# A message stage over 128 pairs of 512 edges under one mask, in place of 232 pairs of 256 edges under four

## The chip, the cores and the metric

The kernel runs on one core of a Trainium2 chip. The metric is the device time of one execution in microseconds (us). TensorE is called PE, VectorE DVE, ScalarE ACT, GpSimd POOL and SyncE SP in the profile.

## What is computed

The whole program is a graph layer, a mixture-of-experts layer, a second graph layer and a second expert layer over 3125 nodes of 256 features, with 53125 edges sorted by their destination. The change concerns the second graph layer's messages:

```
xg0 = y0[edge_src]                       # 64 scalars of the source node
xg1 = y1[edge_src]                       # 64 vectors of 3 components
ea0 = edge_attr[:, :1]
ea1 = edge_attr[:, 1:4]
mid0 = w_a * xg0 * ea0
mid1 = w_b * einsum("euc,ec->eu", xg1, ea1) * INV_SQRT3
mid2 = (w_c * xg0)[:, :, None] * ea1[:, None, :]
mid3 = (w_d * ea0)[:, :, None] * xg1
agg  = segment_sum(concatenate([mid0, mid1, mid2, mid3]), edge_dst)
```

w_a to w_d are 64 weights each per edge, made from edge scalars. Per edge the message has 8 x 64 = 512 values, and they are summed per destination node.

## The kernel before

The stages run one after the other with a barrier between them (times from the profiled span): `sum_neighbours` (0 to 543 us; the first graph layer's sum over neighbours, and the edge weights w with the attributes behind them, 260 columns per edge, written to memory as `edge_w`), the first layer's matmuls and experts (to 1069), `sum_messages` (to 1631), and the update with the second experts (to the end). Nodes lie in 25 tiles of P = 125; the sum over a tile's edges is a matmul on PE whose stationary operand is a mask (edge on the partition, node of the tile in the column).

`sum_messages`. Edges are taken in blocks of SB = 256 (KC = 2 chunks of 128 on the partitions), NB = 208 blocks. A block can touch two tiles, so the work is a list of NPAIR = 208 + 24 = 232 (block, tile) pairs; the tables `pair_need` (the block), `pair_tile` and `pair_dst` (per edge the node's place in the tile) are worked out on the chip at the start of `sum_neighbours`. Two pairs (four chunks) make a step, NST = 116 steps. All operands are float32, and the trace shows every float32 matmul as two instructions. In a step:
- SP loads two blocks of weights `msg_w` (L1939), into RS = 4 buffers.
- POOL fetches the source nodes' 256 values with one indirect DMA per chunk, `msg_got` (L1963): 416 of them, one after the other, into a ring of 32 blocks, at most 7 blocks ahead of the pairs whose products are made (semaphore `made`).
- DVE makes the mask of the next step (`msg_plain`, L2016, 4 x 125 columns, comparing a row of node numbers in PSUM with `pair_dst`), then per pair three products into `msg_prod`: 256 columns (L2033: first and last weight group times the scalars) and twice 384 (L2035: the two middle groups times the vectors). Three steps behind it adds the two sums from PSUM into `agg` (L2045, 512 columns each, second behind first by the semaphore `added`).
- ACT multiplies the mask of each chunk by each of three attributes: 12 masks `msg_scaled` of 125 columns (L1984).
- PE multiplies plain mask by 256 columns of products (L2001) and the three scaled masks by 128 columns each (L2005), per chunk.

In the buffers of `msg_w`, `msg_plain`, `msg_scaled` and `msg_prod` one is borrowed from `x_sb`, so the trace also has the name `x_sb` in their place.

The tables. After the sorted edges' counts are known, DVE builds the pair tables with three trips to PE (L504 to L517 on PE, L833 to L858 on DVE). Then come the row statistics of the nodes (L814, L817 and L821, "gathered statistics"), of which the one-hot masks and the edge work of that stage follow. In that stage POOL's gathers (L441) of block b >= 32 wait for PE's sum of an earlier pair (L556).

## Time and profile before

| what | us |
|---|---|
| median of 3 runs | 1990.52 |
| lowest, highest run | 1987.57, 1991.15 |
| the profiled execution | 1992.24 |
| its span in the trace | 1990.5 |
| first stage, message stage in the span | 0 to 543, 1069 to 1631 |
| PE, DVE, ACT, POOL busy over the span | 1761.1, 1125.7, 1021.4, 1109.6 |
| mean granted TensorE clock | 0.938 |

The trace is of one execution; it takes 1.7 us more than the median of the runs and 1.7 more than its own span. In the rows below an operation's duration runs from its start to the end of its write, and the next of the same engine can begin before that; the difference of two starts is what an operation takes of the engine.

### The profile page before, as it was taken

To read this page: it belongs to the slowest core of one execution; us is meant where nothing else is said; L and a number is where in the kernel's file an instruction comes from. 1 tells how busy PE (TensorE), PEld (TensorE's weight loads), DVE (VectorE), ACT (ScalarE), POOL (GpSimd) and SP (SyncE) were. 2 spreads that over 40 slices of the span, in tenths; PEclk is the share of its full clock that TensorE was granted. 3 is DMA by queue.
4 is the path that set the end of the run, shared out by engine and by line. 5 is a ranking of instruction groups with operands and counts; after the bars stand their busy time and mean duration, and the time that the engine had idled before them with its cause. 6 is when DMAs were issued, how large, how long until landed. Compare 5 with 4: busy or idle time off the path is not lost. (4 is left out here: it accounts for less than half of the span.)

```text
span 1990.5 us, 38467 instructions
## 1 busy us (share of the span) xinstructions
PE 1761.1 (88%) x9911; PEld 1434.7 (72%) x9911; DVE 1125.7 (57%) x2792; ACT 1021.4 (51%) x3052; POOL 1109.6 (56%) x1499
## 2 busy tenths in 40 slices
PE   2799999999899839999755999999999999995999
PEld 1466666666566729999634899888999887774887
DVE  6644333333411665544494999999999973233122
ACT  5455545555443612322246777777777745552221
POOL 6788888888600014555347888888888830000343
PEclk7899999999999559999977999999999999996999
DMA  8767777778640246667456777777777761564553
GB/s 235 221 214 248 246 238 242 242 238 266 210 153 0 65 103 213 208 212 217 148 126 204 210 218 215 215 214 218 216 213 218 209 172 52 172 188 116 177 176 120
DMA packets 229316, 376.43 MB, mean 189 GB/s; under 512 B 66200, under 2 KB 114427, under 8 KB 229117
## 3 DMA queue, kind: packets, MB, share of 16 engines
q1 hardware_dynamic: 174908, 222.13, 36.8%
q0 software_dynamic: 52224, 150.15, 25.2%
q10 hardware_dynamic: 1984, 1.79, 0.3%
q8 instruction: 89, 1.46, 0.3%
q14 instruction: 111, 0.90, 0.1%
HBM read 275.38 MB, written 99.57 MB: 188 GB/s over the span
## 5 line engine op out<-in xcount | busy, mean ns | idle before, releaser
L1963 POOL DMA_INDIRECT msg_got<-y_dram,block_src x416 | 417.9, 1004 | 101.7 <-issue 93.2
L441 POOL DMA_INDIRECT ffn_w<-xn_dram,block_src x384 | 364.4, 949 | 96.0 <-issue 87.5
L1984 ACT ACTIVATE msg_scaled<-msg_plain,msg_w 128x125 f32<-128x125 f32 x1044 | 312.0, 386 | 95.2 <-DVE msg_plain L2016 95.2
L556 PEld LDWEIGHTS sum_ps_bank<-ffn_w,sum_onehot 128*125 128x125 f32 x928 | 171.6, 193 | 191.1 <-issue 175.4
L556 PE MATMUL sum_ps_bank<-ffn_w,sum_onehot 128*125 x928 | 254.3, 399 | 50.0 <-DVE sum_onehot L898 26.1
L886 DVE TENSOR_TENSOR agg<-sum_ps_bank,agg 125x256 f32 x232 | 98.6, 425 | 282.9 <-PE sum_ps_bank L556 278.4
L655 ACT ACTIVATE sum_space<-sum_ps_bank,sum_rec 128x128 f32<-128x128 f32 x416 | 130.1, 364 | 202.1 <-PE sum_ps_bank L543 200.4
L543 PE MATMUL sum_ps_bank<-sum_fc,sum_space 128*128 128x512 f32 x416 | 211.5, 593 | 1.3 <-ACT sum_space L644 1.3
L2005 PEld LDWEIGHTS msg_ps_z<-msg_prod,msg_scaled 128*125 128x125 f32 x1416 | 174.5, 189 | 6.8
L2005 PE MATMUL msg_ps_z<-msg_prod,msg_scaled 128*125 128x128 f32 x1416 | 175.2, 274 | 0.0
L2045 DVE TENSOR_TENSOR agg<-msg_ps_z,agg 125x512 f32 x232 | 159.8, 689 | 22.0 <-DVE agg L2045 1.8
L1538 ACT ACTIVATE ffn_run_hid<-ffn_run_ps_h,cols 128x128 f32<-128x128 f32 x256 | 73.0, 368 | 179.2 <-PE ffn_run_ps_h L1495 179.2
L2462 POOL DMA_INDIRECT last_rows<-ffn_rows,ffn_token x32 | 30.8, 962 | 231.8 <-SPq L78 222.4
L2001 PE MATMUL msg_ps_z<-msg_prod,msg_plain 128*125 128x256 f32 x472 | 126.9, 392 | 20.2 <-ACT msg_scaled L1984 10.8
L1495 PEld LDWEIGHTS ffn_run_ps_h<-ffn_run_rows_t,ffn_run_w 128*128 128x128 f32 x1024 | 125.9, 194 | 5.0 <-DVE ffn_run_rows_t L1580 1.8
L1495 PE MATMUL ffn_run_ps_h<-ffn_run_rows_t,ffn_run_w 128*128 128x128 f32 x1024 | 126.6, 278 | 1.0 <-DVE ffn_run_rows_t L1580 1.0
L1600 POOL DMA_INDIRECT ffn_results<-ffn_run_res,ffn_place x64 | 66.5, 1038 | 102.0 <-DVE ffn_run_res L1559 102.0
L1509 PE MATMUL ffn_run_ps_r<-ffn_w,ffn_run_hid 128*128 x512 | 121.0, 380 | 0.0
L1984 ACT ACTIVATE x_sb<-x_sb 128x125 f32<-128x125 f32 x348 | 104.0, 386 | 33.1 <-DVE x_sb L2016 33.1
L2035 DVE TENSOR_TENSOR msg_prod<-msg_w,msg_got 128x384 f32<-128x384 f32 x236 | 120.4, 551 | 0.1
L2423 PE MATMUL last_ps_r<-wd,last_hid_t 128*128 x512 | 117.7, 384 | 0.0
L2001 PEld LDWEIGHTS msg_ps_z<-msg_prod,msg_plain 128*125 128x125 f32 x472 | 80.2, 190 | 36.1 <-issue 15.3
(346 smaller groups left out, 3252.5 us busy)
## 6 DMA issues: line engine op xcount, KB each, us to landing
edge_w<-sum_space SPq DMA_DIRECT2D x52, 1040.0 KB, 5.2
msg_w<-edge_w SPq DMA_DIRECT2D x174, 260.0 KB
ffn_run_w<-in_L_ffn_w SPq DMA_DIRECT2D x64, 512.0 KB
x_sb<-edge_w SPq DMA_DIRECT2D x58, 260.0 KB
ffn_rows<-agg SPq DMA_DIRECT2D x25, 448.0 KB
ffn_w<-in_L_ffn_w SPq DMA_DIRECT2D x16, 512.0 KB, 8.7
wd<-in_L_ffn_Wd SPq DMA_DIRECT2D x8, 1024.0 KB, 8.9
msg_got<-y_dram,block_src POOLq DMA_INDIRECT x416, 3.7
```

The lines of the kernel that those rows point to most:

```text
L441: pool.indirect_dma_start(got[:, (b + 1) % RING, u, :], None, k.x if b < RAW else k.xn_dram, bass.IndirectOffsetOnAxis(ap=k.block_src[:, b ...
L543: pe.matmul(ps_w[q % WB][:, :, :].rearrange("p u d -> p (u d)"), hid[g % 2][:, b, :], fc2[:, :, :, :].rearrange("p u k v -> p (u k v)"), s ...
L556: last = pe.matmul(ps_sum[n % ZB][0:P, :], onehot[n % OB][:, u, :], got[:, ds(need % RING, 1), u, :].rearrange("p o d -> p (o d)"), start= ...
L655: act.activation(to[:, b, u, 0:128], ps_w[q % WB][:, u, 0:128], ACT.Copy, scale=r[:, b, u, 8:9])
L1495: last = pe.matmul(ps_h[b][c // 4][:, c % 4, :], w1[s][:, q, c * 128:(c + 1) * 128], rows_t[b][:, q, :], start=(q == 0), stop=(q == 1))
L1509: last = pe.matmul(ps_r[b][:, :], hid[b][:, c, :], m.w2[:, ds(e, 1), c, :].rearrange("p o d -> p (o d)"), start=(c == 0), stop=(c == HC - 1))
L1963: pool.indirect_dma_start(got[:, (b + 1) % RING, u, :, :].rearrange("p k v -> p (k v)"), None, k.y_dram, bass.IndirectOffsetOnAxis(ap=k.bl ...
L1984: last = act.activation(scaled[s % MB][:, x, c, :], plain[s % MB][:, c, :], ACT.Copy, scale=w[s % RS][:, c, D + x:D + x + 1])
L2001: pe.matmul(z[0:P, 0:4, :], mask[:, c, :], p[:, c, 0:4, :], start=(u == 0), stop=False, skip_group_check=True)
L2005: last = pe.matmul(z[0:P, 4:6 + x:1 + x, :], by[:, x, c, :], p[:, c, 4 + x:8:3 - x, :], start=False, stop=(x == 2 and u == KC - 1), skip_g ...
L2035: last = dve.tensor_tensor(p[:, at, 3 * q - 2:3 * q + 1, :], v[:, at, q:q + 1, :].to_broadcast([128, KC, 3, MUL]), y[:, :, 1:4, :], ALU.mult)
L2045: dve.tensor_tensor(row(k.agg, tile), ps_z[n % ZB][0:P, :, :].rearrange("p k v -> p (k v)"), row(k.agg, tile), ALU.add)\
```

## The change

Blocks of the message stage are now 512 edges (four chunks): NB4 = 104 blocks, NP4 = 104 + 24 = 128 pairs, and each pair is one unit of work. There is one mask per chunk, the plain one that DVE makes, and PE multiplies it by all 512 columns of products in one matmul of one bank (L2079 in the changed file). What the scaled masks did is done on the products:
- For the three column groups of mid2, ACT copies the product w_c times scalars (64 columns per chunk) three times with an attribute as scale: 12 copies of 64 columns (`split`), in place of 12 masks of 125.
- For mid1, DVE multiplies vectors by attributes in one operation of 768 columns into a new buffer `msg_along` (L2106), adds the three components (two adds of 256 columns, L2113 and L2116), and multiplies by w_b (256 columns, L2120). These wait for one another with the semaphore `along_made`.
- For mid3, one product of 768 columns (L2114); mid0 and the input of the split, one of 512 (L2104).

The add into `agg` is one of 512 columns per unit (L2127), three units behind. POOL's gathers are the same 416, into a ring of 16 four-chunk blocks; it waits only every 8 blocks, for the unit `block4_done` says. SP has one DMA per unit. The memset of agg's first half is moved ahead of the wait for the row of node numbers. The tables for 104 blocks and 128 pairs are made from the old ones' counts in `sum_neighbours`, before the first gathered statistics; PE's edge work and ACT's copies of edge attributes now wait for them (`tables_made` 4). The old tables live on as buffers of that stage only.

```diff
--- before.py
+++ after.py
+NB4 = NB // 2
+NP4 = NB4 + T - 1
+CH = 2 * KC
+RING4, HOLD4 = 16, 8
...
+            pe.wait_ge(four_ready, 5)
+            for h in range(2):
+                pe.matmul(ps_four[:, h:h + 1], ranks.rearrange("p k j -> p (k j)"), minus[:, h:h + 1], start=True, stop=(h == 0))
+            pe.matmul(ps_four[:, 1:2], k.ones[:, :], minus[:, 0:1], start=False, stop=True)
...
+            pe.wait_ge(shifted, 4)
+            pe.wait_ge(chosen_made, 6)
+            for c in range(CH):
+                for h, (at, n) in enumerate(HALVES):
+                    last = pe.matmul(ps_field4[:, c, :], dst_fb[h][0:n, :, c % KC], chosen_half[c // KC][0:n, h, :],
+                                     start=(h == 0), stop=(h == 1))
+            last.then_inc(field_ready, 1)
...
+                        pe.wait_ge(tables_made, 4)
...
+            chain(dve.tensor_tensor(tile4_row[0:1, :], ps_rows4[0:1, 128:128 + NP4], k.iota[0:1, 0:NP4], ALU.add))
+            dve.tensor_scalar(k.pair4_need[0:1, :], ps_rows4[0:1, 0:NP4], float(NB4 - 1), 1.0, ALU.min, ALU.add).then_inc(step, 1)
+            dve.tensor_scalar(k.pair4_tile[0:1, :], tile4_row[0:1, :], float(T - 1), None, ALU.min).then_inc(tables_made, 1)
+            done[0] += 1
+            dve.tensor_copy(k.block4_done[0:1, :], ps_rows4[0:1, 256:256 + NB:2]).then_inc(tables_made, 1)
+            dve.wait_ge(field_ready, 2)
+            dve.scalar_tensor_tensor(k.pair4_dst[:, :, :].rearrange("p n c -> p c n"),
+                                     k.iota[:, 0:NP4].unsqueeze(1).to_broadcast([128, CH, NP4]), float(-P),
+                                     ps_field4[:, :, :], ALU.mult, ALU.add).then_inc(tables_made, 1)
+            dve.wait_ge(tables_made, 4)
...
-            for s in range(NST):
-                if s >= RS:
-                    sp.wait_ge(made, s - RS + 1)
-                    sp.wait_ge(scaled_made, s - RS + 1)
-                if s == 1:
+            for n in range(NP4):
+                if n >= RS:
+                    sp.wait_ge(made, n - RS + 1)
+                    sp.wait_ge(split_made, n - RS + 1)
+                if n == 1:
                     sp.wait_ge(k.x_put, 32 * (NG - 1))
-                for h in range(2):
-                    n = 2 * s + h
-                    need = sp.value_load(k.pair_need[0:1, n:n + 1], min_val=1, max_val=NB)
-                    sp.dma_start(w[s % RS][:, KC * h:KC * h + KC, :].rearrange("p u w -> p (u w)"),
-                                 k.edge_w[ds((need - 1) * SB, SB), :].rearrange("(p u) w -> p (u w)", u=KC)).then_inc(w_in[s % RS], 16)
+                need = sp.value_load(k.pair4_need[0:1, n:n + 1], min_val=1, max_val=NB4)
+                sp.dma_start(w[n % RS][:, :, :].rearrange("p (h u) w -> p h (u w)", h=2),
+                             k.edge_w[ds((need - 1) * (2 * SB), 2 * SB), :].rearrange("(h p u) w -> p h (u w)", h=2, u=KC))\
+                  .then_inc(w_in[n % RS], 16)
...
-                if b > AHEAD:
-                    pool.wait_ge(made, (b - AHEAD + 1) // 2)
+                if b >= 2 * RING4 and b % (2 * HOLD4) == 0:
+                    last = b // 2 - HOLD4 - 1
+                    done = pool.value_load(k.block4_done[0:1, last:last + 1], min_val=1, max_val=NP4)
+                    pool.wait_ge(made, done)
+                    pass_on(pool, freed)
                 for u in range(KC):
                     pool.indirect_dma_start(
-                        got[:, (b + 1) % RING, u, :, :].rearrange("p k v -> p (k v)"), None, k.y_dram,
-                        bass.IndirectOffsetOnAxis(ap=k.block_src[:, b, u:u + 1].bitcast(U32), axis=0)).then_inc(got_in[b % RING], 16)
+                        got[:, (b // 2 + 1) % RING4, b % 2 * KC + u, :, :].rearrange("p k v -> p (k v)"), None, k.y_dram,
...
-            for s in range(NST):
-                act.wait_ge(masked, s + 1)
-                act.wait_ge(w_in[s % RS], 32 * (s // RS + 1))
-                if s >= MB:
-                    act.wait_ge(summed, s - MB + 1)
+
+            def split(n):
+                act.wait_ge(w_in[n % RS], 16 * (n // RS + 1))
+                act.wait_ge(opened, n + 1)
+                p = prod[n % XB]
                 for c in range(CH):
                     for x in range(3):
-                        last = act.activation(scaled[s % MB][:, x, c, :], plain[s % MB][:, c, :], ACT.Copy,
-                                              scale=w[s % RS][:, c, D + x:D + x + 1])
-                last.then_inc(scaled_made, 1)
+                        last = act.activation(p[:, c, 5 + x, :], p[:, c, 8, :], ACT.Copy, scale=w[n % RS][:, c, D + x:D + x + 1])
+                last.then_inc(split_made, 1)
+
+            for n in range(NP4):
+                split(n)
 
         @block.tensor
         def _(pe):
             pe.matmul(ps_lanes[:, :], k.onesf[0:1, :], k.iota[0:1, 0:P], start=True, stop=True).then_inc(lanes_made, 1)
-            for s in range(NST):
-                pe.wait_ge(scaled_made, s + 1)
-                pe.wait_ge(made, s + 1)
-                if s >= ZB // 2:
-                    pe.wait_ge(added, 1 + 2 * (s - ZB // 2 + 1))
-                mask, by, p = plain[s % MB], scaled[s % MB], prod[s % XB]
-                for h in range(2):
-                    z = ps_z[(2 * s + h) % ZB]
-                    for u in range(KC):
-                        c = KC * h + u
-                        pe.matmul(z[0:P, 0:4, :], mask[:, c, :], p[:, c, 0:4, :], start=(u == 0), stop=False, skip_group_check=True)
-                    for x in range(3):
-                        for u in range(KC):
-                            c = KC * h + u
-                            last = pe.matmul(z[0:P, 4:6 + x:1 + x, :], by[:, x, c, :], p[:, c, 4 + x:8:3 - x, :],
-                                             start=False, stop=(x == 2 and u == KC - 1), skip_group_check=True)
+            for n in range(NP4):
+                pe.wait_ge(masked, n + 1)
+                pe.wait_ge(made, n + 1)
+                pe.wait_ge(split_made, n + 1)
+                if n >= ZB:
+                    pe.wait_ge(added, 1 + n - ZB + 1)
+                for c in range(CH):
+                    last = pe.matmul(ps_z[n % ZB][0:P, :, :], plain[n % MB][:, c, :], prod[n % XB][:, c, 0:8, :],
+                                     start=(c == 0), stop=(c == CH - 1))
                 last.then_inc(summed, 1)
 
         @block.vector
         def _(dve):
-            def mask(s):
-                if s == 1:
+            def place(n):
+                return dve.value_load(k.pair4_need[0:1, n:n + 1], min_val=1, max_val=NB4)
+
+            def mask(n):
+                if n == 1:
                     dve.wait_ge(k.x_put, 32 * (NG - 1))
-                if s >= MB:
-                    dve.wait_ge(summed, s - MB + 1)
-                dve.tensor_tensor(plain[s % MB][:, :, :], ps_lanes[:, :].unsqueeze(1).to_broadcast([128, CH, P]),
-                                  k.pair_dst[:, 2 * s:2 * s + 2, :].rearrange("p n u -> p (n u)").unsqueeze(2)
-                                  .to_broadcast([128, CH, P]), ALU.is_equal).then_inc(masked, 1)
-
-            def place(n):
-                return dve.value_load(k.pair_need[0:1, n:n + 1], min_val=1, max_val=NB)
-
-            def products(s, need):
-                p = prod[s % XB]
-                v = w[s % RS][:, :, 0:D].rearrange("p c (k v) -> p c k v", v=MUL)
-                dve.wait_ge(w_in[s % RS], 32 * (s // RS + 1))
-                dve.wait_ge(blocks_in, need[1])
-                if s >= XB:
-                    dve.wait_ge(summed, s - XB + 1)
-                for h in range(2):
-                    y = got[:, ds(need[h] % RING, 1), :, :, :].rearrange("p o u k v -> p (o u) k v")
-                    at = slice(KC * h, KC * h + KC)
-                    dve.tensor_tensor(p[:, at, 0:8:7, :], v[:, at, 0:4:3, :], y[:, :, 0:1, :].to_broadcast([128, KC, 2, MUL]), ALU.mult)
-                    for q in (1, 2):
-                        last = dve.tensor_tensor(p[:, at, 3 * q - 2:3 * q + 1, :], v[:, at, q:q + 1, :].to_broadcast([128, KC, 3, MUL]),
-                                                 y[:, :, 1:4, :], ALU.mult)
-                last.then_inc(made, 1)
+                if n >= MB:
+                    dve.wait_ge(summed, n - MB + 1)
+                dve.tensor_tensor(plain[n % MB][:, :, :], ps_lanes[:, :].unsqueeze(1).to_broadcast([128, CH, P]),
+                                  k.pair4_dst[:, n, :].unsqueeze(2).to_broadcast([128, CH, P]), ALU.is_equal).then_inc(masked, 1)
+
+            def open_products(n, need):
+                p, t = prod[n % XB], along[n % TB]
+                v = w[n % RS][:, :, 0:D].rearrange("p c (k v) -> p c k v", v=MUL)
+                y = got[:, ds(need % RING4, 1), :, :, :].rearrange("p o c k v -> p (o c) k v")
+                dve.wait_ge(w_in[n % RS], 16 * (n // RS + 1))
+                dve.wait_ge(blocks_in, need)
+                if n >= XB:
+                    dve.wait_ge(summed, n - XB + 1)
+                dve.tensor_tensor(p[:, :, 0:9:8, :], v[:, :, 0:4:3, :], y[:, :, 0:1, :].to_broadcast([128, CH, 2, MUL]), ALU.mult)\
+                   .then_inc(opened, 1)
+                dve.tensor_tensor(t[:, :, :, :], y[:, :, 1:4, :],
+                                  w[n % RS][:, :, D:D + 3].unsqueeze(3).to_broadcast([128, CH, 3, MUL]), ALU.mult).then_inc(along_made, 1)
+                return v, y
+
+            def close_products(n, v, y):
+                p, t = prod[n % XB], along[n % TB]
+                dve.wait_ge(along_made, 3 * n + 1)
+                dve.tensor_tensor(t[:, :, 0, :], t[:, :, 0, :], t[:, :, 1, :], ALU.add).then_inc(along_made, 1)
+                dve.tensor_tensor(p[:, :, 1:4, :], v[:, :, 1:2, :].to_broadcast([128, CH, 3, MUL]), y[:, :, 1:4, :], ALU.mult)
+                dve.wait_ge(along_made, 3 * n + 2)
+                dve.tensor_tensor(t[:, :, 0, :], t[:, :, 0, :], t[:, :, 2, :], ALU.add).then_inc(along_made, 1)
+                if n + 1 < NP4:
+                    mask(n + 1)
+                dve.wait_ge(along_made, 3 * n + 3)
+                dve.tensor_tensor(p[:, :, 4, :], v[:, :, 2, :], t[:, :, 0, :], ALU.mult).then_inc(made, 1)
```

DVE in the message stage of the kernel before, one step from its mask to the next: L2060 and L2021 (L2139 and L2086 in the changed file) are loads of table entries into registers, ISA rows are register instructions; rows that repeat are left out.

```order
L2016 TENSOR_TENSOR msg_plain<-msg_ps_lanes,pair_dst 128x500
L2033 TENSOR_TENSOR msg_prod<-msg_w,msg_got 128x2x2x64
L2035 ISA
L2035 TENSOR_TENSOR msg_prod<-msg_w,msg_got 128x2x192 x2
L2060 TENSOR_LOAD pair_tile
L2021 TENSOR_LOAD pair_need
L2021 ISA x2
L2045 ISA
L2045 TENSOR_TENSOR agg<-msg_ps_z,agg 125x512
```

(The second and third row stand there twice, once per pair, and the last row too.) The same engine in the changed kernel, one unit from its first product:

```order
L2104 TENSOR_TENSOR msg_prod<-msg_w,msg_got 128x4x2x64
L2106 ISA
L2106 TENSOR_TENSOR msg_along<-msg_got,msg_w 128x768
L2086 TENSOR_LOAD pair_need
L2086 ISA x2
L2127 ISA
L2127 TENSOR_TENSOR agg<-msg_ps_z,agg 125x512
L2113 TENSOR_TENSOR msg_along<-msg_along 128x4x64
L2114 TENSOR_TENSOR msg_prod<-msg_w,msg_got 128x4x192
L2116 TENSOR_TENSOR msg_along<-msg_along 128x4x64
L2093 TENSOR_TENSOR msg_plain<-msg_ps_lanes,pair_dst 128x500
L2120 TENSOR_TENSOR msg_prod<-msg_w,msg_along 128x4x64
```

Six products of 256 and 384 columns, two adds and a mask for two pairs have become eight operations for one unit, with the add now in the middle of it and the next mask ahead of the last product.

DVE in the first stage of the kernel before, where the tables end and the gathered statistics begin:

```order
L870 CAST iota_h<-sum_space 128x256
L814 BN_STATS ffn_w<-ffn_w 128x6 x4
L817 BN_AGGR ffn_w<-ffn_w 128x2 x4
L814 BN_STATS ffn_w<-ffn_w 128x6 x4
L817 BN_AGGR ffn_w<-ffn_w 128x2 x4
L821 RECIPROCAL ffn_w<-ffn_w 128x4
```

The same place in the changed kernel, its last part; between the cast of iota_h and these rows stand 14 others with two of the three trips to PE:

```order
L935 SCALAR_TENSOR_TENSOR sum_space<-iota,sum_space 128x128 x2
L937 TENSOR_SCALAR sum_space<-sum_space 128x2
L939 TENSOR_SCALAR sum_space<-sum_space 128x256
L939 TENSOR_SCALAR sum_space<-sum_space 80x256
L941 TENSOR_SCALAR sum_space<-sum_space 128x256
L943 TENSOR_TENSOR sum_space<-sum_space 128x256
L945 TENSOR_TENSOR sum_space<-sum_ps_bank,iota 1x128
L946 TENSOR_SCALAR pair_need<-sum_ps_bank 1x128
L947 TENSOR_SCALAR pair_tile<-sum_space 1x128
L949 CAST block_done<-sum_ps_bank 1x104
L951 SCALAR_TENSOR_TENSOR pair_dst<-iota,sum_ps_bank 128x4x128
L855 BN_STATS ffn_w<-ffn_w 128x6 x4
```

The statistics of L814 (now L855) have moved behind all of them.

## Rows read from the trace of the kernel before

**Rows 1.** Windows: stretch; length, busy us (count) per engine; PEclk, DMA share, GB/s
```profile
core 0: us, PE busy (x) PEld busy (x) DVE busy (x) ACT busy (x) POOL busy (x), PEclk, DMA share, GB/s
0.00:543.00 543.00, 470.50 (x1846) 306.54 (x1846) 234.31 (x647) 275.82 (x870) 425.68 (x635) 0.96 0.77 237
1069.00:1631.00 562.00, 533.72 (x3716) 489.71 (x3717) 523.94 (x1047) 421.51 (x1393) 446.73 (x624) 0.98 0.73 214
80.00:100.00 20.00, 15.97 (x58) 9.36 (x56) 12.23 (x29) 0.00 (x0) 13.25 (x20) 1.00 0.60 169
```

**Rows 2.** Timeline, VectorE, a step: start, length, line, operation, out<-in, shape, count
```profile
1299.77 0.69 DVE L2045 TENSOR_TENSOR agg<-msg_ps_z,agg 125x512 f32 x1
1300.38 0.67 DVE L2016 TENSOR_TENSOR msg_plain<-msg_ps_lanes,pair_dst 128x500 f32<-128x500 f32 x1
1300.96 0.42 DVE L2033 TENSOR_TENSOR x_sb<-msg_w,msg_got 128x256 f32<-128x256 f32 x1
1301.31 1.01 DVE L2035 TENSOR_TENSOR x_sb<-msg_w,msg_got 128x384 f32<-128x384 f32 x2
1302.25 0.41 DVE L2033 TENSOR_TENSOR x_sb<-msg_w,msg_got 128x256 f32<-128x256 f32 x1
...
1303.52 1.52 DVE L2045 TENSOR_TENSOR agg<-msg_ps_z,agg 125x512 f32 x2
1304.96 0.67 DVE L2016 TENSOR_TENSOR x_sb<-msg_ps_lanes,pair_dst 128x500 f32<-128x500 f32 x1
```

**Rows 3.** POOL's gathers: group of the page, then first and last in the timeline
```profile
L1963 POOL DMA_INDIRECT msg_got<-y_dram,block_src x416 | 417.9, 1004 | 101.7 <-issue 93.2
...
1069.72 1.04 POOL L1963 DMA_INDIRECT msg_got<-y_dram,block_src  x1 [4.00 <-POOLq L82]
...
1613.09 0.96 POOL L1963 DMA_INDIRECT msg_got<-y_dram,block_src  x1 [0.31 <-issue]
```

**Rows 4.** Timeline, PE: a pair of the message stage; 512 columns in the first stage
```profile
1300.61 1.10 PE L2001 MATMUL msg_ps_z<-msg_prod,msg_plain 128*125 128x256 f32 x4
1301.55 1.47 PE L2005 MATMUL msg_ps_z<-msg_prod,msg_scaled 128*125 128x128 f32 x12
...
505.41 1.02 PE L543 MATMUL sum_ps_bank<-sum_fc,sum_space 128*128 128x512 f32 x2
506.27 1.03 PE L556 MATMUL sum_ps_bank<-ffn_w,sum_onehot 128*125 x4
```

**Rows 5.** Timeline, ACT: the scaled masks of one step
```profile
1301.08 3.59 ACT L1984 ACTIVATE msg_scaled<-msg_plain,msg_w 128x125 f32<-128x125 f32 x12 [0.98 <-DVE msg_plain L2016]
```

**Rows 6.** Timeline, VectorE: first products, second step's wait, last products, last adds
```profile
1077.77 0.42 DVE L2033 TENSOR_TENSOR msg_prod<-msg_w,msg_got 128x256 f32<-128x256 f32 x1 [0.29 <-POOLq L1957]
...
1082.89 0.42 DVE L2033 TENSOR_TENSOR msg_prod<-x_sb,msg_got 128x256 f32<-128x256 f32 x1 [1.83 <-POOLq L1957]
...
1620.76 1.02 DVE L2035 TENSOR_TENSOR msg_prod<-msg_w,msg_got 128x384 f32<-128x384 f32 x2
...
1628.98 1.53 DVE L2045 TENSOR_TENSOR agg<-msg_ps_z,agg 125x512 f32 x2 [1.12 <-PE msg_ps_z L2005]
```

**Rows 7.** Groups by form: VectorE's operation of 768 columns in another stage
```profile
L1708 DVE TENSOR_TENSOR table_got<-table_got 125x768 f32<-125x768 f32 x1 | 1.0, 958 | 2.1 <-DMA table_got<-ffn_results 2.1
```

**Rows 8.** Timeline, first stage: the table work, and POOL's gathers behind it
```profile
17.92 0.17 DVE L714 TENSOR_SCALAR sum_space<-sum_space 128x4 f32<-128x4 f32 x1
18.13 0.17 DVE L715 TENSOR_SCALAR sum_space<-sum_space 128x4 f32<-128x4 f32 x1
...
21.42 1.70 PE L510 MATMUL sum_ps_bank<-sum_space,onesf 128*1 128x232 f32 x4 [2.36 <-DVE sum_space L846]
...
24.61 1.85 PE L517 MATMUL sum_ps_bank<-sum_space 128*128 128x232 f32 x8
...
42.81 0.18 DVE L821 RECIPROCAL ffn_w<-ffn_w 128x4 f32<-128x4 f32 x1 [0.95 <-ACT ffn_w L608]
...
95.48 0.95 POOL L441 DMA_INDIRECT ffn_w<-xn_dram,block_src  x1 [3.79 <-PE sum_ps_bank L556]
...
535.49 0.95 POOL L441 DMA_INDIRECT ffn_w<-xn_dram,block_src  x1 [0.31 <-issue]
```

More of the change, by code:

```diff
@@ new lines, in _ @@
+            dve.tensor_copy(first_tile[:, :], tiles[:, 0, :]).then_inc(four_ready, 1)
+            dve.tensor_reduce(even[:, :], k.ident[:, 0:128:2], AX.X, ALU.add).then_inc(step, 1)
+            done[0] += 1
+            chain(dve.scalar_tensor_tensor(both[:, :], tiles[:, 0, :], -1.0, tiles[:, 1, :], ALU.add, ALU.add))
+            dve.scalar_tensor_tensor(minus[:, :], both[:, :], even[:, 0:1], tiles[:, 1, :], ALU.mult, ALU.subtract).then_inc(four_ready, 1)
+            dve.wait_ge(starts_ready, 2)
@@ new lines, in _ @@
+            chain(dve.tensor_scalar(first4[:, :], ps_four[:, 0:2], -1.0, None, ALU.mult))
+            dve.scalar_tensor_tensor(next4[:, :], ps_four[:, 2:4], -1.0, first4[:, :], ALU.mult, ALU.add).then_inc(step, 1)
+            done[0] += 1
+            chain(dve.tensor_tensor(offset4[:, :], ps_four[:, 4:6], first4[:, :], ALU.subtract))
+            dve.tensor_scalar(even_offset[:, :], offset4[:, :], even[:, 0:1], None, ALU.mult).then_inc(four_ready, 1)
+            for h in range(2):
+                dve.tensor_scalar(past4[:, h, :], k.iota[:, 0:NP4], next4[:, h:h + 1], None, ALU.is_ge).then_inc(past_made, 1)
@@ new lines, in _ @@
+            chain(dve.tensor_tensor(moved[:, :], offset[:, :], offset4[:, :], ALU.subtract))
+            for h in range(2):
+                dve.wait_ge(past_made, h + 3)
+                dve.scalar_tensor_tensor(chosen4[:, h, :], k.iota[:, 0:NP4], first4[:, h:h + 1], past4[:, h, :], ALU.is_ge, ALU.subtract)\
+                   .then_inc(chosen_made, 1)
+            chain(dve.tensor_scalar(moved[:, :], moved[:, :], float(P), None, ALU.mult))
+            for h, (at, n) in enumerate(HALVES):
+                dve.tensor_scalar(dst_fb[h][0:n, :, :], dst_fb[h][0:n, :, :], moved[0:n, h:h + 1], None, ALU.add).then_inc(shifted, 1)
@@ L883, in add_sum @@
             def add_sum(n):
-                tile = dve.value_load(k.pair_tile[0:1, n:n + 1], min_val=0, max_val=T - 1)
+                tile = dve.value_load(pair_tile[0:1, n:n + 1], min_val=0, max_val=T - 1)
                 dve.wait_ge(summed, n + 1)
@@ L1968, in _ @@
                 pool.memset(rest[:, :], 0.0).then_inc(rested, 1)
-                if b % 2 == 1 and b >= 3:
+                if b % 2 == 1 and b >= LAG:
                     arrived(b - 3, b - 2)
```

126 lines of the change are left out of this document (75 added, 51 removed).

## The prediction

> **What bounds the kernel now.** I read the stretches first, then one step of the message stage on each engine, then its two ends. Stages run one after the other, so what the message stage loses, the whole kernel loses. In that stage (1069 to 1631 us) PE is busy 533.7, VectorE 523.9 and POOL 446.7 of 562 us [rows 1]: no bar is full, and busy time alone does not name the bound. The clock granted to TensorE there is 0.98, its upper level (2.4 GHz).
>
> VectorE's step shows what it could do. Reckoned from start to start [rows 2]: mask to product 0.58 (1300.38 to 1300.96), product of 256 columns 0.35, two of 384 columns 0.94 (0.47 each), first add to second 0.83, second add to the next mask 0.61; the whole step 4.58 (1300.38 to 1304.96). 116 such steps are 531 us. From the first product's start to the last one's end it took 1621.78 - 1077.77 = 544.0 us [rows 6]. The gathers on POOL explain the rest: 416 of them start from 1069.72 to 1613.09, 543.4 us or 1.31 each, and the idle time in front of most of them is only their own issue [rows 3]; VectorE at times waits for them, as by 1.83 us in the second step [rows 6]. So POOL's gathers pace the stage, VectorE follows with 13 us in hand, and PE (0.94 for four instructions of 256 columns and near 1.3 for twelve of 128, twice per step, so about 4.5 of 4.68) is no further off [rows 4]. After the last product come 8.73 us of PE and adds (1621.78 to 1630.51) [rows 6].
>
> **The change: VectorE's unit.** 232 pairs of 256 edges in 116 steps become 128 pairs ("units") of 512 edges, 104 blocks plus 24 tile borders. Per unit VectorE now issues one mask of 500 columns, one add of 512, one product of 512, two operations of 768 and three of 256 (two adds, one product).
> - Mask 0.58 and add 0.61, as in [rows 2]; there is one add per unit, so the add-behind-add time of 0.83 is gone.
> - 512 columns: from 256 to 384 the step grew by 0.12 to 0.13, so 0.60.
> - 768 columns: the same growth gives 0.34 + 4 x 0.13 = 0.86. The one operation of that size in the trace lasts 0.958 [rows 7]; a 384 lasts 0.55 and takes 0.47, so the next one starts 0.08 before its end, which gives 0.88. I take 0.87, two are 1.74. That one of them multiplies by a value repeated over 64 columns is taken to cost nothing; no row shows such an operand from SBUF, the mask's repeated operand from PSUM costs nothing visible (500 columns 0.58).
> - Three of 256: 1.02.
> Sum 4.55. Bounds: 4.4 if wide operations grow a little more slowly, 4.7 if 768 cost their whole 0.96.
>
> 128 x 4.55 = 582.4. The first three units have no add (-1.8), the last makes no mask (-0.6), the last operation ends 0.1 after its step. At the start the gathers are slower than VectorE: a block of 512 edges needs four gathers, 5.0 to 5.2 us [rows 3], the first units 3.94 (no add) and then 4.55; tile borders, where one block serves two units, come from the fifth unit on. Four units starve by about 1 us each: +4. From there VectorE uses 4.55 x 128/104 = 5.60 per block against 5.24, so POOL runs ahead to its new hold (every 8 blocks it waits until the ring's old half has been used) and is never late again. From first product to last: 584.1 against 544.0, **+40.1**. POOL's wait stands in front of gathers alone and at least 7 gathered blocks stay unused then, so it costs nothing.
>
> **What hides the rest.** PE: eight instructions of 512 columns take 0.43 each ((506.27 - 505.41)/2) [rows 4], 3.44 per unit, under 4.55. ACT: twelve copies of 64 columns instead of twelve of 125 which take 3.59 [rows 5]; at most 3.6 per unit, and they start after the unit's first product, so they are over before VectorE's last product of the unit is. Sums are read three units later. SP has one DMA per unit for two per step, with four buffers as before. The new waits of VectorE on itself each have another operation in between: the add into agg before the first small add, the 768-column product before the second, the next unit's mask before the last product. If that cover were missing, each would cost 0.83 - 0.61 = 0.22 [rows 2].
>
> **Tail.** The last unit leaves 3.44 of PE, a fraction for the handover, and one add of 0.69: 4.4 for 8.73, **-4.3**. Before, the last step alone had PE work of 4.5 and the step before was still in PE.
>
> **Tables.** Before the first gathered statistics of the first stage VectorE now runs 26 operations and waits for PE three times, and everything behind (statistics, first one-hot mask, PE's edge work, which now waits for the tables too) is late by that. Start to start a small one of such a chain takes 0.21 [rows 8]. Until the first PE trip seven operations, 1.6; trip 0.5; up to the marks of all pairs 1.9; then PE has 28 instructions of 128 columns. Those of 232 took 1.70 for 4 and, later, 1.85 for 8 [rows 8], so 0.24 or 0.13 for 128: 6.6 or 3.6, I take 5, with VectorE's own work there hidden; last, 0.75 for the 512-column result. Together 9.7 (8.3 to 11.4). Of it 0.95 is saved where VectorE waited for ACT at 42.81 [rows 8]. Is it passed on? POOL's gather at 95.48 waited 3.79 us for PE's sums, and from there to 535.49 it paces the stage without a pause [rows 8]; PE, 80% busy at 80 to 100 us [rows 1], can win back up to some 3 us of a delay by then. I take **+8**, bounds 3 and 11.
>
> **Sum.** 40.1 - 4.3 + 8 = +43.8. The profiled execution took 1992.24, so 2036.0; it is 1.7 above the median of the runs, which gives 2034.
>
> **Rivals.**
> - *VectorE's waits on itself are exposed.* One to three of them per unit at 0.22 [rows 2]: 28 to 84 us more, 2062 to 2118. For it: the two adds of a step, which depend on one another, do pay it. Against it: here each has 0.34 to 0.87 us of other work between. Chance 0.10.
> - *Operations do not overlap.* A unit of whole durations: 0.67 + 0.69 + 0.69 + 2 x 0.96 + 3 x 0.42 = 5.23, x 128 = 669, or 86 us above my sum: 2120. The rows speak against it: a 384 lasts 0.55 and the next starts after 0.47 [rows 2]. Chance 0.03. The Trainium skill, "VectorE: DVE Perf Modes", section "The DRAIN you can't avoid", says that a VectorE operation does not start until the pipe of the one before is empty. Taken as whole durations back to back that is this rival; the trace, with 0.08 of overlap in each step, disagrees with it here.
> - *PE falls to its lower clock.* With one burst of 3.44 in every 4.55 us its idle gaps become regular. At 1.2 GHz a unit would be 6.9 on PE, 128 are 881, about 300 more: 2330. Against it: at 80 to 100 us PE is busy 15.97 of 20 with gaps of the same kind and the clock stays 1.00, and over the first stage it is 0.96 at 470.5 of 543 [rows 1]. Chance 0.02.
> - *The other side: not slower.* The stage stays bound by the gathers if a unit costs VectorE less than 544/128 = 4.25, that is 0.30 less than my sum: the 768s at 0.72 instead of 0.87. Then the stage costs only its tail's -4.3 and the tables: 1994 with +8, 1986 if PE makes up for the tables. For it: only one row has 768 columns, and none starts another operation straight behind it. Against: 256, 384 and the 512-column add (0.61) lie on one line. Chance 0.03.
> - The forecast itself: 0.82.
>
> **The range.** The forecast by itself: 4.4 per unit is 19 below, 4.7 is 19 above, tables -5 and +3; most of that is 2015 to 2056, more likely in its middle. With a chance of 0.10 for one or more exposed waits, the upper end goes to 2062, one wait per unit. I give 2020 to 2062. A measurement of this kernel tells some 0.2% (4 us) from nothing; faster by that 0.02, within it 0.03, slower 0.95.
>
> **What the changed profile would show.** VectorE busy without gaps in the message stage, with a start-to-start unit of 4.55; gaps on POOL every 32 gathers with the waits named for VectorE's products; PE at clock 0.98 or above with a gap of about 1 us per unit; first to last product near 584 us, message stage near 598; the first stage 8 us longer with the gap before its first gathered statistics. I am wrong if the start behind a 768 comes after clearly less or more than 0.87, if an operation behind a wait on VectorE itself shows idle time, if POOL's new hold lets VectorE run dry after the ring turns, or if the first stage does not grow.

## The result, and the profile after

The changed kernel takes 2077.88 us (median of 4 runs, 2076.98 to 2079.95) against 1990.0 (4 runs, 1987.57 to 1991.15): ratio 1.0445, 95% interval 1.0427 to 1.0463. Slower, as forecast, but by 88 us where 43.8 were forecast.

The span grows from 1990.5 to 2075.7, and two traces side by side say where. First work of the second stage on PE: 543.97 before, 554.15 after, +10.2. First gather of the message stage (1081.15, against [rows 3]): a further +1.3. From there to the first product +2.6. First product to last one: 624.4 against 544.0 [rows 6], **+80.4**. End of the last product to end of the last add: 4.6 against 8.73, -4.1. The rest is 5.0 shorter. Together +85.2.

Windows of the changed kernel, first stage, message stage and the end (busy us and count of each engine, granted clock, DMA share, GB/s), to be held against [rows 1]:

```profile
core 0: us, PE busy (x) PEld busy (x) DVE busy (x) ACT busy (x) POOL busy (x), PEclk, DMA share, GB/s
0.00:554.00 554.00, 477.86 (x1879) 312.21 (x1879) 241.31 (x675) 276.73 (x870) 426.31 (x636) 0.96 0.75 232
1081.00:1721.00 640.00, 488.12 (x1026) 190.31 (x1024) 594.71 (x1027) 385.98 (x1537) 529.04 (x624) 0.95 0.64 196
1721.00:2075.00 354.00, 318.96 (x1885) 265.50 (x1885) 99.57 (x283) 131.90 (x254) 63.55 (x64) 0.95 0.47 146
```

In the message stage POOL has the same 624 instructions as in [rows 1], and is busy 529 us instead of 447. Nothing of the diff gave POOL more to do. Two groups of the page of the changed kernel name them (busy us, mean ns of one, idle us before them):

```profile
L2042 POOL DMA_INDIRECT msg_got<-y_dram,block_src x416 | 500.2, 1202 | 101.7 <-issue 97.3
...
L2079 PE MATMUL msg_ps_z<-msg_prod,msg_plain 128*125 128x512 f32 x520 | 247.5, 620 | 80.2 <-DVE msg_prod L2120 80.2
```

A gather takes 1.202 us on average, 1.004 in [rows 3]. With the 0.30 of issue between them, 416 need 626.3 us from first to last start (543.4 before): the stage is still paced by the gathers, and the gathers have become longer.

Timeline of the changed kernel, VectorE and POOL in order of time, a little more than one unit (start, length, engine, line; the time after the arrow-bracket is idle time before it; "..." stands for POOL's short memsets, ScalarE and PE):

```profile
1404.83 0.95 DVE L2114 TENSOR_TENSOR msg_prod<-msg_w,msg_got 128x768 f32<-128x768 f32 x1
1404.99 1.61 POOL L2042 DMA_INDIRECT msg_got<-y_dram,block_src  x1 [0.17 <-issue]
1405.70 0.42 DVE L2116 TENSOR_TENSOR msg_along<-msg_along 128x256 f32<-128x256 f32 x1
1406.03 0.67 DVE L2093 TENSOR_TENSOR x_sb<-msg_ps_lanes,pair_dst 128x500 f32<-128x500 f32 x1
1406.62 0.41 DVE L2120 TENSOR_TENSOR msg_prod<-msg_w,msg_along 128x256 f32<-128x256 f32 x1
1406.91 0.94 POOL L2042 DMA_INDIRECT msg_got<-y_dram,block_src  x1 [0.30 <-issue]
...
1408.15 0.95 POOL L2042 DMA_INDIRECT msg_got<-y_dram,block_src  x1 [0.17 <-issue]
1408.34 0.69 DVE L2104 TENSOR_TENSOR x_sb<-x_sb,msg_got 128x512 f32<-128x512 f32 x1 [1.31 <-issue]
1408.95 0.95 DVE L2106 TENSOR_TENSOR msg_along<-msg_got,x_sb 128x768 f32<-128x768 f32 x1
...
1409.41 1.31 POOL L2042 DMA_INDIRECT msg_got<-y_dram,block_src  x1 [0.30 <-issue]
...
1410.87 0.95 DVE L2114 TENSOR_TENSOR x_sb<-x_sb,msg_got 128x768 f32<-128x768 f32 x1
1411.03 1.62 POOL L2042 DMA_INDIRECT msg_got<-y_dram,block_src  x1 [0.17 <-issue]
...
1412.99 0.68 DVE L2104 TENSOR_TENSOR msg_prod<-msg_w,msg_got 128x512 f32<-128x512 f32 x1
1413.60 0.95 DVE L2106 TENSOR_TENSOR msg_along<-msg_got,msg_w 128x768 f32<-128x768 f32 x1
...
1414.47 0.68 DVE L2127 TENSOR_TENSOR agg<-msg_ps_z,agg 125x512 f32 x1
```

The reader is to compare the ends. The gather of 1404.99 began 0.16 us into the product of 768 columns (L2114, ends 1405.78) and ended at 1406.60, which is 0.82 after that. The one of 1409.41 lies over L2106, which ends at 1409.90; it ends at 1410.72: 0.82. That of 1411.03 lies over the next L2114, end 1411.82, and ends at 1412.65: 0.83. The gather of 1406.91 began when VectorE's operation (L2120, ends 1407.03) had 0.12 left, that of 1408.15 when VectorE was idle; they take 0.94 and 0.95. The other way round nothing is seen: L2104 at 1408.34 and L2106 at 1408.95 have two SBUF inputs and start while the gather of 1408.15 runs, 0.61 apart as elsewhere. Counted over the trace, 253 of the 416 gathers last over 1.0 us, and 252 of these end 0.82 (within 0.03) after the end of a VectorE operation whose two inputs both lie in SBUF (the other is the stage's first, 1.04 as in [rows 3]). The time over 0.95 adds up to 105 us; in the kernel before, counted in the same way, to 23. The difference, 82, is as large as the growth of the stage, 80.4. The row of 1408.34 shows the other end of it: 1.31 us in which VectorE is idle. The profile names no releaser there; in the program the gathered block is one of three things that L2104 waits for, and that it is the late one is read from the gathers' pace.

The kernel before has the same pattern with smaller holds (timeline, two rows; each of the two operations of 384 columns lasts 0.55):

```profile
1305.87 1.02 DVE L2035 TENSOR_TENSOR msg_prod<-msg_w,msg_got 128x384 f32<-128x384 f32 x2
1305.98 1.27 POOL L1963 DMA_INDIRECT msg_got<-y_dram,block_src  x1 [0.31 <-issue]
```

The first 384 ends at 1306.42, the gather at 1307.25, 0.83 later. There 75 gathers last over 1.0 us, and 74 of them end so.

### The profile page after: what moved, and what is told of

The parts are those of the page before. It is cut to its first block and busy times, and to the rows that moved or that the text cites. A ratio compares the mean times of both kernels' runs of the same rounds, so it can differ in the third digit from the quotient of the medians.

```text
span 2075.7 us, 31977 instructions
## 1 busy us (share of the span) xinstructions
PE 1721.3 (83%) x7256; PEld 1137.8 (55%) x7256; DVE 1203.3 (58%) x2798; ACT 987.7 (48%) x3196; POOL 1191.9 (57%) x1499
## 5 line engine op out<-in xcount | busy, mean ns | idle before, releaser
L2042 POOL DMA_INDIRECT msg_got<-y_dram,block_src x416 | 500.2, 1202 | 101.7 <-issue 97.3
L2079 PE MATMUL msg_ps_z<-msg_prod,msg_plain 128*125 128x512 f32 x520 | 247.5, 620 | 80.2 <-DVE msg_prod L2120 80.2
L2063 ACT ACTIVATE msg_prod<-msg_prod,msg_w 128x64 f32<-128x64 f32 x780 | 193.4, 334 | 126.7 <-DVE msg_prod L2104 126.7
L2079 PEld LDWEIGHTS msg_ps_z<-msg_prod,msg_plain 128*125 128x125 f32 x520 | 96.3, 194 | 229.9 <-issue 104.9
L2079 PE MATMUL msg_ps_z<-x_sb,msg_plain 128*125 128x512 f32 x248 | 120.3, 631 | 34.5 <-DVE x_sb L2120 34.5
L2063 ACT ACTIVATE x_sb<-x_sb,msg_w 128x64 f32<-128x64 f32 x372 | 92.2, 334 | 59.7 <-DVE x_sb L2104 59.7
L2079 PEld LDWEIGHTS msg_ps_z<-x_sb,msg_plain 128*125 128x125 f32 x248 | 46.6, 196 | 107.7 <-issue 50.3
L2500 PEld LDWEIGHTS last_ps_r<-wd,last_hid_t 128*128 128x128 f32 x512 | 95.5, 191 | 11.8
L981 DVE TENSOR_TENSOR sum_onehot<-sum_ps_bank,ffn_table_raw 128x250 f32<-128x250 f32 x232 | 97.0, 418 | 7.7
```

The lines of the kernel that those rows point to most:

```text
L981: dve.tensor_tensor(onehot[n % OB][:, :, :], ps_lanes[:, :].unsqueeze(1).to_broadcast([128, KC, P]), pair_dst[:, n, :].unsqueeze(2).to_bro ...
L2042: pool.indirect_dma_start(got[:, (b // 2 + 1) % RING4, b % 2 * KC + u, :, :].rearrange("p k v -> p (k v)"), None, k.y_dram, bass.IndirectO ...
L2063: last = act.activation(p[:, c, 5 + x, :], p[:, c, 8, :], ACT.Copy, scale=w[n % RS][:, c, D + x:D + x + 1])
L2079: last = pe.matmul(ps_z[n % ZB][0:P, :, :], plain[n % MB][:, c, :], prod[n % XB][:, c, 0:8, :], start=(c == 0), stop=(c == CH - 1))
L2500: last = pe.matmul(ps_r[n % 2][:, 0:D], hid_t[n % 2][:, c, :], k.wd[:, ds(e, 1), c, :].rearrange("p o d -> p (o d)"), start=(c == 0), stop ...
```

## The experiments

Two theories after the result. **A:** a gather that starts while VectorE runs an operation with two SBUF inputs is held until it ends; wide operations hold long. **B:** the gathers are slower for another reason in the change: weights in loads of 520 KB, the ring of 16 with its hold, the new order. A third, that VectorE waits for itself, is a rival of the prediction. In all runs the "kernel before" was measured on the same chip.

**Both 768s with one input from PSUM.** The changed kernel; weights and attributes replaced by a row of node numbers of the same shape, so the values are others.

```diff
-                                  w[n % RS][:, :, D:D + 3].unsqueeze(3).to_broadcast([128, CH, 3, MUL]), ALU.mult).then_inc(along_made, 1)
+                                  ps_lanes[:, 0:3 * CH].rearrange("p (c x) -> p c x", c=CH).unsqueeze(3).to_broadcast([128, CH, 3, MUL]), ALU.mult).then_inc(along_made, 1)
-                dve.tensor_tensor(p[:, :, 1:4, :], v[:, :, 1:2, :].to_broadcast([128, CH, 3, MUL]), y[:, :, 1:4, :], ALU.mult)
+                dve.tensor_tensor(p[:, :, 1:4, :], ps_lanes[:, 0:MUL].unsqueeze(1).unsqueeze(1).to_broadcast([128, CH, 3, MUL]), y[:, :, 1:4, :], ALU.mult)
```

> The changed kernel, but both operations of 768 columns take their second operand from PSUM (the row of node numbers) instead of the weights and attributes in SBUF, so their values are wrong and their sizes the same. Theory A: a gather on POOL that starts while VectorE runs an operation with two SBUF inputs is held until that operation ends, and a 768 holds it up to 0.95 - 0.13 = 0.82 us. Then the mean gather falls from 1.20 to under 1.02, 416 of them need under 555 us, VectorE is the bound at 128 x 4.54 = 581 and a few more, 40 less than the 624.4 measured: 2038 (2032 to 2044). Theory B: the gathers are slower for another reason (weights loaded in pieces of 520 KB, the new ring and its hold), whatever VectorE reads: 2078, within 4.

Measured 2047.01, ratio 1.0275 (1.026 to 1.0291): 31 us less than the changed kernel, with the same loads, ring and order. B alone had 2078, so it falls. A had 2038 (2032 to 2044) and missed by 9: the mean gather is 1.122 us, not under 1.02. The group of its gathers, and rows of its timeline:

```profile
L2042 POOL DMA_INDIRECT msg_got<-y_dram,block_src x416 | 466.8, 1122 | 101.6 <-issue 91.8 <-DMA msg_got<-y_dram,block_src 6.3 <-POOLq L88 3.5
...
1402.50 0.41 DVE L2120 TENSOR_TENSOR msg_prod<-msg_w,msg_along 128x256 f32<-128x256 f32 x1
1402.64 1.70 POOL L2042 DMA_INDIRECT msg_got<-y_dram,block_src  x1 [0.30 <-issue]
1402.84 0.68 DVE L2104 TENSOR_TENSOR msg_prod<-msg_w,msg_got 128x512 f32<-128x512 f32 x1
...
1405.24 0.95 DVE L2114 TENSOR_TENSOR msg_prod<-msg_ps_lanes,msg_got 128x768 f32<-128x768 f32 x1
1405.90 0.95 POOL L2042 DMA_INDIRECT msg_got<-y_dram,block_src  x1 [0.31 <-issue]
```

None of the 134 gathers that start in one of the PSUM-fed 768s is held. But 82 of the 107 that start in L2120 end 0.82 or 0.83 after L2104, the next operation (1402.64 + 1.70 = 1404.34, L2104 ends at 1403.52): a gather can miss the change from one to the next. In all, 133 gathers last over 1.0 us, and 132 of them end so after an operation with two SBUF inputs.

**Each 768 as two of 384, all in SBUF.**

```diff
+                for h in (slice(0, KC), slice(KC, CH)):
+                    dve.tensor_tensor(p[:, h, 1:4, :], v[:, h, 1:2, :].to_broadcast([128, KC, 3, MUL]), y[:, h, 1:4, :], ALU.mult)
```

(and the same for `msg_along`.)

> The changed kernel with each operation of 768 columns cut into two of 384, all inputs in SBUF as before. Theory A: the longest hold is 0.55 - 0.13 = 0.42 in place of 0.82, the mean gather falls to 1.05 to 1.13, so 416 take 565 to 600 us; VectorE's unit grows by 2 x 0.07 to 4.68, 599 for 128 and a few more; the longer of the two is some 603 against 624.4: 2057 (2048 to 2064), although VectorE has more to do. Theory B: gathers as slow as now, VectorE's extra work hidden under them: 2078. If VectorE itself were the bound (third theory: waits on itself), 18 us are added: 2096.

Measured 2097.36, ratio 1.0534 (1.0515 to 1.0553): A in that form missed by 40, and the time is the one of the third theory (2096). The trace says that the agreement is luck: if VectorE were the bound it would not stand idle before L2104, as it does 36 times for 26.8 us together, and the mean gather is 1245 ns, more than the 1202 of the wide form, which gives 416 gathers 643.9 us. Timeline of this kernel:

```profile
1399.47 0.68 DVE L2104 TENSOR_TENSOR x_sb<-msg_w,msg_got 128x512 f32<-128x512 f32 x1
...
1399.75 2.17 POOL L2042 DMA_INDIRECT msg_got<-y_dram,block_src  x1 [0.17 <-DMA msg_got<-y_dram,block_src]
1400.07 1.02 DVE L2107 TENSOR_TENSOR msg_along<-msg_got,msg_w 128x384 f32<-128x384 f32 x2
...
1401.01 0.68 DVE L2130 TENSOR_TENSOR agg<-msg_ps_z,agg 125x512 f32 x1
...
1401.94 1.02 DVE L2117 TENSOR_TENSOR x_sb<-msg_w,msg_got 128x384 f32<-128x384 f32 x2
1402.22 1.89 POOL L2042 DMA_INDIRECT msg_got<-y_dram,block_src  x1 [0.30 <-issue]
1402.88 0.41 DVE L2119 TENSOR_TENSOR msg_along<-msg_along 128x256 f32<-128x256 f32 x1
1403.21 0.67 DVE L2093 TENSOR_TENSOR msg_plain<-msg_ps_lanes,pair_dst 128x500 f32<-128x500 f32 x1
```

The gather of 1399.75 ends at 1401.92, 0.83 after the end of both halves (1401.09), where the add with a PSUM input follows; that of 1402.22 ends at 1404.11, 0.82 after L2119 (1403.29), where the mask follows. So a hold can last to the end of an unbroken run of operations with two SBUF inputs. Shorter operations back to back are no gap. Counted over this trace, 182 gathers are held and 181 of them end 0.82 after such an operation; the time over 0.95 is 123 us. Gathers that begin at the same place of a run (0.27 us into L2117) are let in at its first end in some cases and at its last in others; no run here shows what decides it.

**No operation of the unit with two SBUF inputs.** As the first experiment, and L2104, both small adds and L2120 take one operand from the same row in PSUM too.

```diff
-                dve.tensor_tensor(t[:, :, 0, :], t[:, :, 0, :], t[:, :, 1, :], ALU.add).then_inc(along_made, 1)
+                dve.tensor_tensor(t[:, :, 0, :], t[:, :, 0, :], ps_lanes[:, 0:MUL].unsqueeze(1).to_broadcast([128, CH, MUL]), ALU.add).then_inc(along_made, 1)
```

> The changed kernel with one operand of every product and of both small adds taken from PSUM (the row of node numbers), so that no VectorE operation of a unit has two SBUF inputs; values wrong, sizes the same. Theory A, as the first runs have left it: a gather is held until the end of the operation with two SBUF inputs that runs when it starts, or of a later one of the same unbroken run. Without any such operation every gather takes 0.95, 416 need some 523 us, and VectorE's 128 x 4.54 = 581 and a few for the start bound the stage: first to last product 583 to 587, total 2036 to 2042. If VectorE, POOL or the loads have another limit in this stage the window stays at e1's 590 or more.

Measured 2030.4, ratio 1.0194 (1.0162 to 1.0226): A's direction, and 6 below its range of 2036 to 2042. The group of the gathers, and one of POOL's rows:

```profile
L2042 POOL DMA_INDIRECT msg_got<-y_dram,block_src x416 | 394.9, 949 | 122.5 <-issue 91.9 <-DVE msg_prod L2120 15.3 <-DVE x_sb L2120 6.0
```

```profile
1449.80 0.95 POOL L2042 DMA_INDIRECT msg_got<-y_dram,block_src  x1 [5.09 <-DVE msg_prod L2120]
```

Of 416 gathers 415 take 0.94 to 1.0 (the first takes 1.04). POOL now runs ahead and waits at its hold for VectorE's last product, five times in the stage, 21 us in all, and VectorE bounds it: 576.6 from first product to last (1092.67 to 1669.25), 4.50 per unit. That is the course that the prediction took for the changed kernel itself, at 8 less than its 584. So the gathers' holds cost this change about 624.4 - 576.6 = 48 us, and VectorE's own longer list 33. The cut between the two is good to some 5 us: with an operand in PSUM the operations are a little shorter themselves (a unit 4.50 against 4.54, 5 us over 128).

**The wide operation alone, in the kernel before.** The two products of 384 of a pair as one of 768 (it reads other weights than the reference; same columns). Everything else as before.

```diff
-                    for q in (1, 2):
-                        last = dve.tensor_tensor(p[:, at, 3 * q - 2:3 * q + 1, :], v[:, at, q:q + 1, :].to_broadcast([128, KC, 3, MUL]),
-                                                 y[:, :, 1:4, :], ALU.mult)
+                    last = dve.tensor_tensor(p[:, at, 1:7, :].rearrange("p c (q x) v -> p c q (x v)", q=2),
+                                             v[:, at, 1:4, :].rearrange("p c x v -> p c (x v)").unsqueeze(2).to_broadcast([128, KC, 2, 3 * MUL]),
+                                             y[:, :, 1:4, :].rearrange("p c x v -> p c (x v)").unsqueeze(2).to_broadcast([128, KC, 2, 3 * MUL]), ALU.mult)
```

> The kernel before, with the two products of 384 columns of a pair made as one of 768 (same columns and buffers; the weights it reads are the wrong ones); masks, PE and ACT work, gathers and loads as before. VectorE saves 2 x 0.07 per step. Theory A: a gather that starts early in a 768 is held up to 0.82 in place of 0.42, the mean gather of 1.004 grows by 0.02 to 0.07, 8 to 29 us: 1998 to 2020. Theory B (the gathers of the changed kernel were slow for its loads, its ring or its hold): VectorE has less to do, 1986 to 1992.

Measured 2006.76 against 1989.8 on that chip, ratio 1.008 (1.0057 to 1.0103), in A's range. VectorE has 232 instructions and 16 us of occupation less (two of 384 take 2 x 0.47, one of 768 takes 0.87), and the kernel is slower by 17 us: the mean gather is 1050 ns against 1004, and 0.046 x 416 = 19 us.

```profile
L1963 POOL DMA_INDIRECT msg_got<-y_dram,block_src x416 | 436.6, 1050 | 101.5 <-issue 95.7 <-POOLq L82 4.0 <-DMA msg_got<-y_dram,block_src 1.8
```

**The tables alone, in the kernel before.** VectorE's 26 operations, PE's matmuls and the new waits of the first stage; their result is not used.

```diff
             dve.wait_ge(iota_made, 2)
+            dve.wait_ge(ident_made, 1)
+            dve.wait_ge(tri_made, 1)
+            dve.tensor_copy(ranks, k.tri[:, 0:128:2].unsqueeze(2).to_broadcast([128, 64, 2])).then_inc(four_ready, 1)
...
+            dve.wait_ge(tables_made, 4)
```

> The kernel before with only the new tables made at the start of the first stage (same operations, same waits, into memory that is not used afterwards), message stage as before. If the 10.2 us by which the first stage ends later are the tables': 2000 (1998 to 2002). If they belong to something else of the change (other positions of the edge-attribute copies, tile names, the clock): under 1994.

Measured 2000.41 against 1991.32, ratio 1.0044 (1.003 to 1.0057): +9.1, as expected. So the first stage's growth in the changed kernel is the tables'.

**One weight group in PSUM, in the kernel before.** This is theory A the other way round: in the old stage the gathers pace too, so a hold less is time gained. ScalarE copies one group of weights (256 columns per step) into the free PSUM bank behind its masks.

```diff
+                if s >= 1:
+                    act.wait_ge(made, s)
+                act.activation(ps_v[:, :, :], w[s % RS][:, :, 2 * MUL:3 * MUL], ACT.Copy).then_inc(v_copied, 1)
                 last.then_inc(scaled_made, 1)
...
+                dve.wait_ge(v_copied, s + 1)
...
+                        vq = v[:, at, q:q + 1, :] if q == 1 else ps_v[:, at, :].unsqueeze(2)
```

> The kernel before, with one of its two weight groups for the 384-column products copied to PSUM by ScalarE (256 columns per step), so that two of the four products of 384 have one SBUF input; everything computed as before. Theory A: gathers there last 1.004 on average against 0.95 unhindered; half of that goes, 416 x 0.03 = 11 us of the gather pace, and VectorE's own 531 stays below: 1978 to 1984. Theory B: no gain, and with the ScalarE copy (some 0.45 in a step where ScalarE has 1 us left) and its waits 1990 or more.

Measured 1979.09 against 1991.32, ratio 0.993 (0.9916 to 0.9944): faster by 0.7%, in A's range. Its gathers take 974 ns on average, the copy 0.36 us of ScalarE, and the window from first to last product is 530.8 against 544.0.

**The mask between the adds.** On top of it, the first copy is issued before the first scaled masks, and the next mask stands between the two adds.

```diff
-                if s + 1 < NST:
-                    mask(s + 1)
...
+                if s + 2 < NST:
+                    mask(s + 2)
                 if s >= 3:
                     add_sum(second, tile[1])
```

> The version with one weight group in PSUM, its first copy issued ahead of the first scaled masks (3.6 us of the start), and the next mask made between the two adds of a step, so that the second add no longer pays 0.22 for the first: VectorE's step 4.36, 506 us for 116, its gathers (0.974 each, 530 us) the bound again, PE's 4.5 per step (522) close. Computes the reference. Expected 3 us at the start and 0 to 5 in the stage below that version's 1979: 1971 to 1977. If the mask there waits for PE (it needs the sums one step earlier than before): 1980 or more.

Measured 1987.56 against 1989.8, ratio 0.9986 (0.9969 to 1.0003), where 1971 to 1977 were expected: a miss, the gain of the version before it is gone. Where nothing is waited for, VectorE's step is shorter (1301.92 to 1306.23 from mask to mask, 4.31, against 4.56), but the mean gather is 996 ns instead of 974, and over the stage (538.7 us, 116 steps) a step takes 4.64. The gathers fall on other operations: 53 start in a product of 256 columns and 29 of these are held, against 30 and 3 in the version before. Whether the length of the step or the order of its operations moved them was not tried apart.

**Both weight groups in PSUM.** The same order, and 512 columns per step copied, so that only the products of 256 columns have two SBUF inputs (the cut is against the version with the mask between the adds).

```diff
-                        vq = v[:, at, q:q + 1, :] if q == 1 else ps_v[:, at, :].unsqueeze(2)
+                        vq = ps_v[:, at, q - 1:q, :]
```

> As the version with the mask between the adds, and both weight groups of the 384-column products copied to PSUM (512 columns per step on ScalarE, some 0.6 us where it has 0.9 left). Only the products of 256 columns can hold a gather, up to 0.29. Theory A: the mean gather 0.95 to 0.96, 416 need 523 to 527; PE's 4.5 per step is as much: 1966 to 1974. If ScalarE becomes too late for the next step's products: over 1979.

Measured 1968.44 against 1989.8, ratio 0.9892 (0.987 to 0.9914), in the expected range of 1966 to 1974: the fastest kernel of the study, and faster than both kernels of the change. Groups and windows of it:

```profile
L1965 POOL DMA_INDIRECT msg_got<-y_dram,block_src x416 | 397.8, 956 | 100.7 <-issue 88.7 <-DMA msg_got<-y_dram,block_src 7.5 <-POOLq L82 3.1
```

```profile
1081.00:1604.00 523.00, 506.57 (x3663) 476.08 (x3664) 502.02 (x1035) 471.98 (x1504) 419.73 (x615) 0.99 0.75 221
```

The stage has shrunk to the gathers' own pace, 523.1 us from first product to last for 416 x 1.258, with the granted clock at 0.99 and VectorE, PE and ScalarE all over 90% busy. PE, at 97%, is so near its own bound that this run alone would not tell which of the two it is.

## Why the prediction was right or wrong

- *What bounds the kernel before* was read rightly: POOL's gathers pace the message stage. The run with one weight group in PSUM confirms it: VectorE's operations are the same in number and length, the gathers are 12.7 us shorter in all (417.9 to 405.2 busy), and first product to last is 13.2 us shorter.
- *VectorE's unit of 4.55* was right: 1412.99 to 1417.53 in an undisturbed unit is 4.54, 512 columns take 0.61 (1412.99 to 1413.60) and 768 take 0.87 (1413.60 to 1414.47).
- *The step that failed* is the sentence "From there VectorE uses 4.55 x 128/104 = 5.60 per block against 5.24, so POOL runs ahead ... and is never late again". It took the gathers' pace as a property of POOL. [rows 3] had a mean of 1004 ns where single gathers of the first stage last 0.95 [rows 8]; that difference of 0.05 was the hold, there to be read, and it depends on VectorE's operations. With the changed ones a block of four gathers takes 626.3/104 = 6.02, above VectorE's 5.60, and the stage 624.4 instead of 584.1. The term +40.1 was +80.4: about 33 of it are VectorE's (576.6 against 544.0), about 48 are holds. This miss of 40.3 is nearly the whole difference between the 43.8 forecast and the 85.2 by which the span grew. The rest of the sum was sound: with the holds taken away the changed kernel takes 2030.4 against 1989.8, +40.6.
- *The rivals.* None was this one. VectorE's waits on itself are not exposed: in the rows above each operation behind such a wait starts without idle time. Operations overlap as in [rows 2]: 768 columns last 0.95 and take 0.87. (The section that the prediction names from the Trainium skill, "VectorE: DVE Perf Modes", "The DRAIN you can't avoid", adds that a next operation which is not held starts earlier, so the overlap does not speak against the skill.) PE did not fall to its lower level for the stage: the granted clock was 0.95 in the stage. But that is under the "0.98 or above" of the prediction's signs; in stretches of 40 us from 1121 on it lies between 0.91 and 1.00, where the kernel before has 1.00 from 1109 on. PE stands idle for 0.86 to 2.37 us before each unit between 1400 and 1420, waiting for VectorE's last product, so this cost the stage nothing there. The other side, in which the stage stays at the gathers' pace, had the right bound and the wrong assumption that this pace is 544.
- *Tail*: -4.1, forecast -4.3. The last PE work, 3.67 for 3.44, and one add are what is left.
- *Tables*: +10.2 in the trace and +9.1 by themselves in the kernel before, forecast +8 with bounds 3 and 11. The work was sized well (9.7; the first one-hot mask moved from 47.03 to 56.94, 9.9); too much was taken for recovered: nothing was. The timeline of the changed kernel has the gather that stood at 95.48 [rows 8] at 106.48, behind a wait for PE of 9.19 in place of 3.79:

```profile
106.48 0.95 POOL L457 DMA_INDIRECT ffn_w<-xn_dram,block_src  x1 [9.19 <-PE sum_ps_bank L596]
```

- *Not foreseen*: +1.3 before the first gather, +2.6 from there to the first product, and -5.0 behind the message stage, where PE's granted clock is 0.95 and was 0.93 before. Their causes were not tried.

## What to carry to other kernels

Where GpSimd issues many gathers, look at the spread of their durations before taking their pace as fixed: if some end a constant time after VectorE operations with two SBUF inputs, the gathers are held by them. Then wider VectorE operations, or several such back to back, can cost more than they save (17 us for the first, 19 us more for the second in the runs above); an operand in PSUM, copied there by an engine that has time, takes the hold away. A change that lengthens VectorE's list in a stage where it has 13 us in hand needs its sum first, before any question of overlap: that alone made this one slower.

## What the runs showed of the hardware

A gather of 128 rows takes 0.95 us on POOL when nothing holds it, and ends 0.82 after the operation that held it (252 of 253, 181 of 182 and 132 of 133 gathers over 1.0 us in the changed kernel, the halved one and the one with both 768s from PSUM). The Trainium skill, "SBUF — State Buffer", section "SBUF: two separate sides", says that VectorE and GpSimd share one pair of ports under an exclusive lock which an operation with two SBUF inputs takes against a GpSimd operation that reads SBUF, and that whichever starts first has it while the other fully blocks. For VectorE first and the gather second these traces agree: a mean gather of 1202 ns with two SBUF inputs in all products and small adds, 949 with none. For the gather first they show no such block: 119 of the changed kernel's 128 operations L2106 start while a gather that is not held runs, and start 0.60 us after L2104 like the others. Port and lock themselves are not in a trace; what the runs show is who is held, by which operations, and how long.

The halved kernel shows that a hold can pass over the change from one operation to the next: 2.17 us for a gather over three operations of which the longest lasts 0.68. What the gathers meet changed too when the mask was put between the adds: they were held for 0.046 on average, and for 0.024 in the version before.
